# Attention in a two-layer kernel: the fills of the key and query stacks move from the head of POOL's and DVE's programs into their first three turns

## The reference

```python
q = (hidden_states @ Wq.T + bq).reshape(b, s, HEADS, HEAD_DIM)
k = (hidden_states @ Wk.T + bk).reshape(b, s, HEADS, HEAD_DIM)
v = (hidden_states @ Wv.T + bv).reshape(b, s, HEADS, HEAD_DIM)
q = q * SCALE
scores = jnp.einsum('bqhd,bkhd->bhqk', q, k)
probs = jax.nn.softmax(scores.astype(jnp.float32), axis=-1).astype(scores.dtype)
out = jnp.einsum('bhqk,bkhd->bqhd', probs, v).reshape(b, s, d)
return out @ Wo.T + bo
```

## Time and profile before

| what | value |
|---|---|
| median of 3 runs | 1046.87 us (1046.27 to 1047.94) |
| span of the profiled execution | 1043.3 us |
| PE busy | 922.4 us, 88% |
| DVE busy | 709.6 us, 68% |
| ACT busy | 641.2 us, 61% |
| POOL busy | 606.1 us, 58% |
| mean granted clock of PE | 0.945 |

### The profile page before, as it was taken

One profiled execution on the slowest core, in us unless ns is written; L12 is line 12 of the kernel. 1 busy time (PEld: TensorE's weight loads), 2 busy tenths in 40 slices (PEclk: granted clock), 3 DMA queues, 4 the chain that ended last, 5 costly groups with the idle time before them and its releaser, 6 DMA issues. The chain is left out here.

```text
span 1043.3 us, 28212 instructions
## 1 busy us (share of the span) xinstructions
PE 922.4 (88%) x9810; PEld 654.9 (63%) x9810; DVE 709.6 (68%) x1511; ACT 641.2 (61%) x1304; POOL 606.1 (58%) x1277
## 2 busy tenths in 40 slices
PE   6999999499989999439999999999999999953766
PEld 5888887289956666325666666666666666532554
DVE  4888887575434444237888888888888888825752
ACT  4777776322224444124788888888888888752552
POOL 4777776277725555564566667676666766434003
PEclk9999999699999999756999999999999999986999
DMA  8600000311122322134344434435443344201000
GB/s 313 281 3 2 3 3 2 109 53 52 52 77 82 83 82 70 46 106 132 115 150 125 143 119 139 135 124 155 128 142 118 118 135 125 75 22 58 13 3 21
DMA packets 66770, 96.84 MB, mean 93 GB/s; under 512 B 10706, under 2 KB 57426, under 8 KB 62162
## 3 DMA queue, kind: packets, MB, share of 16 engines
q1 hardware_dynamic: 61394, 84.00, 25.8%
q0 software_dynamic: 5248, 11.15, 3.3%
HBM read 57.60 MB, written 36.47 MB: 90 GB/s over the span
## 5 line engine op out<-in xcount | busy, mean ns | idle before, releaser
L1373 DVE TENSOR_REDUCE a_neg_max<-a_slot 128x4 f32<-128x1024 f32 x256 | 306.0, 1218 | 86.2 <-PE a_slot L1510 68.3
L1462 ACT ACTIVATE a_pT<-a_slot 128x1024 f32<-128x1024 f32 x256 | 255.4, 1025 | 8.4 <-PE a_slot L1510 5.0
L1543 PE MATMUL a_ps_o<-a_pT,a_v_pad 128*32 128x256 f32 x2048 | 137.9, 387 | 0.0
L1510 PE MATMUL a_slot<-a_k_stack,a_q_stack 62*128 62x256 f32 x1024 | 120.7, 317 | 5.9 <-DMA a_q_stack<-q_dram 3.9
L1510 PE MATMUL a_slot<-a_q_stack,a_k_stack 64*128 64x256 f32 x1024 | 114.4, 312 | 3.7 <-ACT a_pT L1462 1.9
L728 POOL DMA_INDIRECT y_rows<-m_total,m_token x80 | 76.8, 960 | 66.0 <-ACT m_total L881 52.1
L1510 PEld LDWEIGHTS a_slot<-a_k_stack,a_q_stack 62*128 62x128 f32 x1024 | 79.7, 192 | 48.3 <-issue 21.5
L1510 PEld LDWEIGHTS a_slot<-a_q_stack,a_k_stack 64*128 64x128 f32 x1024 | 75.4, 187 | 35.0 <-issue 23.5
L331 DVE TENSOR_TENSOR r_score<-ps_score,r_decay 128x512 f32<-128x512 f32 x128 | 81.4, 678 | 7.7 <-PE ps_score L490 7.6
L1543 PEld LDWEIGHTS a_ps_o<-a_pT,a_v_pad 128*32 128x32 f32 x2048 | 53.6, 109 | 45.8 <-issue 19.4
L830 DVE TENSOR_TENSOR m_hidden_e<-m_gate_e,m_banks 128x512 f32<-128x512 f32 x40 | 27.5, 688 | 76.5 <-ACT m_gate_e L876 76.5
(11 more groups left out here) (292 smaller groups left out, 2054.0 us busy)
## 6 DMA issues: line engine op xcount, KB each, us to landing
a_k_stack<-k_dram SPq DMA_DIRECT2D x64, 256.0 KB, 3.0
a_q_stack<-q_dram SPq DMA_DIRECT2D x64, 256.0 KB, 3.6
k_dram<-a_part SPq DMA_DIRECT2D x64, 128.0 KB, 2.3
q_dram<-a_part SPq DMA_DIRECT2D x32, 256.0 KB, 2.1
sorted_in<-h SPq DMA_DIRECT2D x10, 528.0 KB, 13.7
m_xe<-sorted_in SPq DMA_DIRECT2D x40, 132.0 KB, 2.2
expert_up<-in_eu_dram SPq DMA_DIRECT2D x1, 4096.0 KB, 24.9
out_dram<-e_x_plus_h SPq DMA_DIRECT2D x32, 128.0 KB, 2.1
```

Source lines behind the costliest of these rows:

```text
L1373: nc.vector.tensor_reduce(neg_max[:, p, half, t, :, g], slots[SLOT_OF["m", j]][:].rearrange("p (c r) s -> p c r s", c=TILES), AX.X, ALU.ma ...
L1462: nc.scalar.activation(pT[:, j % PT_RING], slots[SLOT_OF["e", j]][:], ACT.Exp).then_inc(e_read, 1)
L1510: ins = nc.tensor.matmul(slot[:, tile * UT + r], weights[at, n, half, g * UT + r, of_weights].bitcast(F32R), moving[at, n, half, g * UT + ...
L1543: ins = nc.tensor.matmul(ps_o[q * APAD:(q + 1) * APAD, g // 2], v_pad[:, p, t, g * UNIT + q], pT[:, (2 * g + t) % PT_RING, q], start=g % 2 ...
```

## The change

The loop of three fills at the head of POOL's program becomes a step `preset_k_stack` with lag 1, last in POOL's list; the loop at the head of DVE's becomes `preset_q_stack` with lag 1, ahead of `preset_v_pad` at the end of DVE's list. Each step does one buffer, for s below 3. So buffer s is filled at the end of turn s + 1: turns 1, 2 and 3 of a pipeline that begins with turn 0. The operations, their sizes and the waits of SP for them are the same.

```diff
             pool.wait_ge(preset, 3)
-            for n in range(BUFS):
-                nc.gpsimd.memset(k_stack[:, n], 1.0).then_inc(preset_k, 1)
+
+            def preset_k_stack(s, p, r):
+                if s < BUFS:
+                    nc.gpsimd.memset(k_stack[:, s], 1.0).then_inc(preset_k, 1)
...
             pipeline(pool, [(split_max(0), 5), (weigh, 9), (add_given, 0), (inv_std_early, 1), (split_qk(0), 3), (inv_std, 2),
-                            (split_max(1), 5), (split_qk(1), 3), (bias, 5), (pad_v, 4), (inv_std3, 8)], B, B)
+                            (split_max(1), 5), (split_qk(1), 3), (bias, 5), (pad_v, 4), (inv_std3, 8), (preset_k_stack, 1)], B, B)

         @block.vector
         def _(dve):
-            for n in range(BUFS):
-                nc.vector.memset(q_stack[:, n], 0.0).then_inc(preset_q, 1)
             dve.wait_ge(bias_sum, 1)
             nc.vector.tensor_tensor(bo[:], bo[:], ps_misc[:, 0:D], ALU.add)
             nc.vector.tensor_scalar(bq_scaled[:], bq[:], SCALE, None, ALU.mult).then_inc(weights_ready, 1)
+
+            def preset_q_stack(s, p, r):
+                if s < BUFS:
+                    nc.vector.memset(q_stack[:, s], 0.0).then_inc(preset_q, 1)
...
-                           (preset_v_pad, 2)], B, B)
+                           (preset_q_stack, 1), (preset_v_pad, 2)], B, B)
```

## The result

The changed kernel takes 1041.7 us (median of 5 runs, 1041.56 to 1043.75) against 1046.87 (5 runs, 1045.67 to 1047.94). The ratio is 0.9942, with a 95% interval of 0.9924 to 0.9960: 6.1 us less, between 4.2 and 8.0. A second comparison, with 8 and 25 runs, gave 1043.22 against 1047.55, a ratio of 0.9960 (0.9944 to 0.9975): 4.2 us less, between 2.6 and 5.9. So it is faster, by some 5 us. The first ratio times the median before is 1040.8, and the forecast was 1042.4, with a range from 1041.0 to 1044.3: by this comparison the gain came out larger than the 4.5 us of the sum and just beyond the range, by the second it lies inside.

The account below looks back on a forecast made before the run. PE was taken to bound the attention phase, so only an earlier entry, set by fills heading POOL's and DVE's programs, could gain: 5.6 − 0.94 − 0.15 = 4.5 us, 1046.87 to 1042.4, range 1041.0 to 1044.3.

Parts of the forecast that it names:

- The heads: Fills at the start of POOL's and DVE's programs: without them sequence 0's statistics and h come 5.6 us earlier.
- POOL's late fills: Two k_stack fills in POOL's queue before the first split: 0.94 us of their 3.52 stays visible, split at 451.0.
- Rival B: POOL's two late fills before the first split cost nothing: 1041.3 us; chance 0.08.
- The third fill, and DVE's: k_stack's third fill fits POOL's 3.27 us idle before sequence 1's splits; DVE's fills fit its idle time: cost 0.
- Rival C: Fills land in sequence 0's chain, one engine waiting for the other's access: slower, 1048.7 us or more; chance 0.05.
- The DMA term: Stores come up to 0.9 us nearer behind the read into q_stack: costs 0.15 us, bounds 0 and 0.9.
- The clock: PE's clock rise in the attention phase follows the work, to near 484.5: no cost.
- rival A: The rise of PE's clock in the attention phase does not come along with the earlier work; chance 0.14.
- Rival D: The gain is absorbed, by a fixed-time load or a later stage waiting for something outside: 1046.9 us; chance 0.07.
- The time outside the sum: The median of 1046.87 stands 3.6 us above the profiled execution's span of 1043.3; taken to stay.

Follow-up runs that it names:

- the halves alone: The change made on one engine only, the other's three fills left at the head: ratio 1.0015 (POOL's half) and 1.0002 (DVE's half) against the kernel before.
- fillers: Small matmuls, results never read, keeping PE busy at the entry, added to the late fills: ratio 0.9920; carried on through the first scores: 0.9959, against the kernel before.
- held stores: The late fills with SP holding sequence 1's stores until sequence 0's reads landed: ratio 0.9969 against the kernel before; with fillers through the first scores as well: 0.9957.
- POOL's head alone: Only k_stack's fills moved to POOL's turns 1 to 3, q_stack's left at DVE's head: 1049.72 us against 1047.55 for the kernel before, ratio 1.0015.
- the shifted code: 32 do-nothing instructions at the head of PE's program, added to the kernel before: ratio 0.9997; added to the late fills: 0.9949, both against the kernel before.
- DVE's head alone: Only q_stack's fills moved to DVE's turns 1 to 3, k_stack's left at POOL's head: 1047.65 us against 1047.55 for the kernel before, ratio 1.0002.
- the late fills: The changed kernel with k_stack's second and third fill one turn later: 1041.33 us against 1047.55 for the kernel before, ratio 0.9945.

## Where the prediction was right and where it was wrong

**The heads (5.6).** Right: statistics at 442.56 for 442.5, h at 444.87 for 444.8. That both have to go was in the argument only as far as "DVE is the later of the two"; the halves alone show it (−0.43 and 0.00 at the statistics).

**POOL's late fills (−0.94).** The place was right to the digit: 451.00 for 451.0, POOL without idle time ahead of it (2.55 us in the earlier trace rows). But the prediction took a microsecond at the first split for a microsecond at the first score. Removing the visible fill moved the split by 0.90 and the score by 0.15. The count from the statistics says the same: to the first score they took 19.38 to 19.46 us in the three traces in which a late fill holds the split, and 18.74 to 19.73, 19.23 on the average, in the six in which none does (fillers and held stores left aside). So of the 0.94 us only some 0.2 reached the scores. Rival B, whose worth was these 0.94 us, would have come to little: with the fill moved away the phase took 496.8 and 497.0 us, as in the changed kernel.

**The third fill, and DVE's (0).** Right. POOL's wait ahead of the splits of sequence 1 went from 3.27 to 0.63: the fill fitted in. DVE still waits 7.52 us for the first scores. Rival C, that fills hold the other engine, is out: the k_stack fills of the changed trace take 1.81 and 1.80 while a fill of DVE runs beside them, and 1.76 from the start of one to the step behind it, as worked out from the earlier trace rows.

**The DMA term (0.15 off the gain).** This is the step that failed, in size and in sign. The prediction took the stores behind the read for a burden that could only grow as they come nearer, with bounds of 0 and 0.9 us. They came nearer, from 2.37 to 1.48, and the read to score went from 6.06, 5.87 and 5.73 (mean 5.89) to 5.14 and 5.21 (5.18): 0.7 us shorter on the average, 0.92 in the first pair of traces. The range of that term had left out a gain, with no row that excludes one. POOL's head alone shows the same with nothing else gained: split 0.90 later, store spacing 1.47, read to score 5.18, and the first score where it was. So the sum took 0.94 and 0.15 off the gain, where the runs show 0.94 off and 0.7 back on: the split came late, and the read behind it landed the sooner. What makes the landing quick stays open; with the stores held away altogether it was 5.47 and 6.01, so their nearness is not shown to be a burden at all.

**The clock (0).** It was taken to follow the work exactly, with rival A if it did not. In the pair of traces it rose 6.8 us earlier, 1.2 more than the work, which gave 0.5 us; over two traces of the changed kernel and three of the kernel before (one of these with the shifted code), 4.9 us earlier against 5.4 of the work, which cost 0.2. The price of a late rise comes out alike in all nine traces without fillers, each set against the first trace of the kernel before: the first copy of oT moves as the first score does, plus 0.45 us for each us by which the rise moves beyond the score, within 0.04 us. The 0.45 is fitted to these traces. Before to after: −5.59 − 0.45 × 1.17 = −6.12, measured −6.14; DVE's head alone: −1.11 − 0.45 × 0.83 = −1.48, measured −1.50; POOL's head alone: +0.03 + 0.45 × 0.34 = +0.18, measured +0.20. The earlier trace rows give nearly the same: four score matmuls take 0.80 us at a granted clock of 0.50 and 0.50 us at 1.00, so a microsecond of PE-bound work at the low clock loses some 0.4 us. With the rise at 489.0 and the work 4.5 us ahead that would have been 1.8 us lost and a time of 1044.2. The moment of the rise scatters: from the first score to the rise it took 21.6 and 19.3 us in two executions of the same kernel, a difference of 2.3 us. That the rise goes with PE's work the fillers show, with which it came at 8.2 and 3.6 us of the phase, ahead of the first scores (19.8 and 19.2); what fixes its exact moment stays open. Rival A, a rise that stays at 489, is out. Rival D is out as well: the lead at the copies of oT stood at 6.12 to 6.15 us in all 32 sequences.

**The time outside the sum (3.6).** Misread. Time less span is 1.7 to 1.9 us in every run of either kernel. The other 1.8 us of the 3.6 goes, by its size, with the last phase of the profiled execution, which had the highest clock seen there (0.88, 99.13 us). The forecast left it out of the difference, which was right; but the forecast of the span, 1038.8 for 1039.8, took that luck for lasting. The base itself was soft: three runs gave 1046.87, 25 runs of the same kernel 1047.55, from 1044.66 to 1050.88.

**The sum again.** First split 4.66, read to score 0.7 (forecast −0.15), clock −0.2: 5.2 us, against 5.3 for the mean length of the attention phase (502.72, 501.62 and 502.31 against 496.79 and 496.95). The comparisons of times gave 6.1 (4.2 to 8.0) and 4.2 (2.6 to 5.9); 5.3 lies in both intervals, and so does the 4.5 of the forecast. So the mechanism is as predicted, and the term of the reads is what was off: with a gain of 0.7 in its place the sum would have been 5.4. What is left to the 6.1 us, and put the first comparison beyond the range, is scatter as far as the runs show: single traces of the two kernels differ in the attention phase by 4.7 to 5.9 us, depending on which two are compared, and the second comparison, 4.2, errs to the other side.

**Two readings beside the sum.** The dip at the 17th and 18th slice does not end where the attention phase begins: the phase begins at 441.4, and the 18th slice (443 to 469 us) is its entry. And in the earlier trace rows the other engines are busy 30 to 42 of 50 us, not 30 to 44. Neither enters the sum.

## What to carry to other kernels

When two programs feed one join, clear both heads or neither: here the halves were worth nothing that could be measured and the whole 5 us. Follow a gain to the row that paces the stage, through every DMA, since 0.9 us at the splits was 0.15 to 0.2 at the scores; and bound a transfer that you can't see on both sides of zero. Compare a stage by its own length over several traces: a late phase with idle stretches moved the whole by 5 us through the clock alone, as much as the change.

## What the runs showed of the hardware that was not expected

- The last phase, never edited, took 99.1 to 104.8 us as its granted clock went from 0.88 to 0.79:

```profile
944.75:1049.50 104.75, 69.64 (x1380) 54.31 (x1380) 57.49 (x129) 41.63 (x105) 22.12 (x24) 0.79 0.07 22
```

  (the kernel with POOL's head alone). The work on the other engines is the same; PE is busy 5.8 us more than in the 99.13 us.
- Full clock through the entry was worth only 2.1 us of 496.8, and 1.0 of it from the first scores on, while the earlier trace rows would give 0.4 × 20 = 8 for PE-bound work from the first scores at 20.3 to the rise at 40.8 us of the phase with the late fills. So that stretch is PE-bound in a part of it only, the later one, or the fillers, which PE has to do as well, ate the rest; this was not tried by itself.
- Small matmuls that keep PE busy came with a phase 1 to 2 us shorter than without them, or 10 us longer in an execution in which the clock fell among them.
- The same read (two issues of 256 KB) took 5.1 to 6.4 us from its first issue to the matmul that waits for it, in thirteen profiled executions.
